# Weighing the values of two key blocks at a time in a fused attention stage, from six places for exponentials in place of four

## The reference

```python
x = x + 0.5 * moe(layernorm(x))          # top 2 of 8 experts, 256 -> 256 -> 256, silu gate
x = x + attention(layernorm(x))          # 16 heads of 16 features
x = x + 0.5 * moe(layernorm(x))

def attention(x):                        # 16 sequences of 1024 tokens
    latent = (x @ W_k + x @ W_v) @ W_down_kv
    q, k, v = x @ W_q, latent @ W_up_k, latent @ W_up_v
    scores = q @ k.T / sqrt(256) * exp(-0.01 * abs(tq - tk))
    return softmax(scores) @ v @ W_o
```

## Time and profile before

| what | value |
|---|---|
| median of 3 runs | 5893.35 us (5887.23 to 5893.88) |
| span of the profiled execution | 6207.9 us |
| the profiled execution's own time beside the span | not given by the page; the span is the whole of it |
| attention stage in it | from 1260 to 5157 us, 1024 W |
| TensorE busy, whole span | 5474.1 us (88%) |
| VectorE busy | 4582.3 us (74%) |
| ScalarE busy | 3294.6 us (53%) |
| GpSimd busy | 2823.2 us (45%) |

### The profile page before, as it was taken

How to read it: one execution, slowest core, us unless ns; L and a number is a source line. 1 busy time by engine, 2 the same in 40 slices (tenths; PEclk the granted TensorE clock), 3 DMA queues, 4 the chain that set the end, 5 groups by cost and what they waited for, 6 DMA issues and landing times.

```text
span 6207.9 us, 114160 instructions
## 1 busy us (share of the span) xinstructions
PE 5474.1 (88%) x35792; PEld 3260.2 (53%) x35792; DVE 4582.3 (74%) x14351; ACT 3294.6 (53%) x6557; POOL 2823.2 (45%) x2857
## 2 busy tenths in 40 slices
PE   4459999389999999999999999999999996988874
PEld 4448888134444444444444444444444444877763
DVE  6545555577888888888888888888888994545554
ACT  1124444156666666666666666666666664433321
POOL 5650000263656656647557566476574333012244
PEclk9999999689999999999999999999999997999987
DMA  4433333444545554545545555454454443335555
GB/s 152 147 109 105 105 105 102 130 100 89 122 104 113 127 102 117 117 101 121 117 106 123 110 114 123 100 122 113 104 122 96 97 75 121 105 112 160 157 180 171
DMA packets 535036, 728.64 MB, mean 117 GB/s; under 512 B 79892, under 2 KB 450740, under 8 KB 534452
## 3 DMA queue, kind: packets, MB, share of 16 engines
q1 hardware_dynamic: 485300, 587.06, 39.3%
q0 software_dynamic: 49152, 134.28, 7.3%
HBM read 425.64 MB, written 295.44 MB: 116 GB/s over the span
## 4 chain that ended last, share of the span: by engine, by line
PE 76%; DVE 10%; another core or an unknown queue 4%; issue 4%; POOL 3%; ACT 2%; DMA 1%; SPq 1%; DVEq 0%; ACTq 0%; POOLq 0%
PE psum L1312 15%; PE psum L1163 14%; PE psum L395 12%; PE psum L1172 11%; PE psum L412 6%; PE psum L1176 3%; PE psum L403 2%; DVE at_mx L1453 2%; PE psum L384 2%; PE psum L1288 2%; PE psum L1220 2%; ACT at_P L1376 1%; PE psum L1208 1%; PE psum L1230 1%
## 5 line engine op out<-in xcount | busy, mean ns | idle before, releaser
L1376 ACT ACTIVATE at_P<-psum 128x512 f32<-128x512 f32 x4096 | 2131.2, 602 | 1098.5 <-PE psum L1172 577.0
L1453 DVE TENSOR_REDUCE at_mx<-psum 128x4 f32<-128x512 f32 x3584 | 2220.2, 681 | 286.9 <-PE psum L1163 260.5
L1163 PE MATMUL psum<-at_kst,at_qst 96*128 96x128 bf16 (+3 forms) x7168 | 1599.1, 293 | 55.0 <-DVE at_mx L1453 28.8
L1172 PE MATMUL psum<-at_qst,at_kst 99*128 99x512 bf16 (+3 forms) x5120 | 1465.4, 319 | 100.8 <-ACT at_P L1376 96.1
L1163 PEld LDWEIGHTS psum<-at_kst,at_qst 96*128 96x128 bf16 x7168 | 616.3, 99 | 1326.5 <-DVE at_mx L1453 520.7
L1312 PE MATMUL psum<-at_P,at_V 128*17 128x512 f32 x8192 | 1095.2, 607 | 0.0
L1691 POOL TENSOR_TENSOR at_Sd<-at_Sd,at_m 128x1024 f32<-128x1024 f32 x256 | 484.4, 1898 | 886.8 <-DVE at_m L1462 885.9
L1172 PEld LDWEIGHTS psum<-at_qst,at_kst 99*128 99x128 bf16 x5120 | 490.5, 98 | 251.1 <-ACT at_P L1376 129.9
L1176 PE MATMUL psum<-at_ident,at_Sd 128*128 128x128 f32 x2048 | 565.1, 276 | 0.0
L696 POOL DMA_INDIRECT m2Y<-ys,m2yi x256 | 243.9, 953 | 692.2 <-DMA ys<-m2X 370.7
L1448 DVE CUSTOM_DVE_ANT_0 at_Sd<-psum,at_Dm 128x128 f32<-128x128 f32 x2048 | 444.9, 286 | 148.3 <-PE psum L1163 86.5
(11 more groups left out here) (267 smaller groups left out, 7893.0 us busy)
## 6 DMA issues: line engine op xcount, KB each, us to landing
parts<-at_pt SPq DMA_DIRECT2D x768, 128.0 KB
at_qst<-parts SPq DMA_DIRECT2D x768, 128.0 KB
at_kst<-parts SPq DMA_DIRECT2D x128, 384.0 KB
m2X<-xs SPq DMA_DIRECT2D x280, 128.0 KB
ys<-m2X SPq DMA_DIRECT2D x280, 128.0 KB
m1X<-xs SPq DMA_DIRECT2D x264, 128.0 KB
ys<-m1X SPq DMA_DIRECT2D x264, 128.0 KB
at_kst<-parts SPq DMA_DIRECT2D x128, 256.0 KB
```

Of the source, the lines that this page charges most:

```text
L1163: ins = e.matmul(bank[z % 4][:, col - 512 * u:col - 512 * u + ln], self.qst[0:96, s, side, 128 * t:128 * t + 128], self.kst[0:96, s, 1 - s ...
L1172: ins = e.matmul(turns[a % 3][:, q0 - 512 * qh:q0 - 512 * qh + ln], self.kst[0:99, s, side, 128 * kb:128 * kb + 128], self.qst[0:99, s, 1 ...
L1376: e.activation(self.P[:, i % NP, 512 * qh:512 * qh + 512], turns[a % 3], ACT.Exp).then_inc(self.taken.sem, 1)
L1453: e.tensor_reduce(self.mx[:, p % 2, hh, 8 * o + 4 * u:8 * o + 4 * u + 4], of, op=ALU.max, axis=AX.X).then_inc(self.s_read.sem, 1)
```

## The change

A W is done only behind every second step, and then for two blocks: `k = kb - 1` and `k = kb`, eight matmuls (16 records) in a row in place of four. In the numbers of the steps, a W stood behind every step `s` and now stands behind the even ones. `P` gets six places in place of four, so that three blocks of exponentials can be held. The count on the semaphore `weighed` is halved, and all waits on it are rewritten to it. Room for the two new places comes in part from `wk`, which no longer has memory of its own but lies in place 4 of `P` (it is used only while the stage is set up). No other work is moved in the list.

```diff
-    NS, NP, LEAD, DIAG = 3, 4, 4, 7
+    NS, NP, LEAD, DIAG = 3, 6, 4, 7
...
-        self.wq, self.wk, self.wo = sb("wq", [128, 2, D]), sb("wk", [128, 2, D]), sb("wo", [128, 2, D])
+        self.wq, self.wo = sb("wq", [128, 2, D]), sb("wo", [128, 2, D])
+        self.wk = self.P[:, 4, 0:512].rearrange("p (k d) -> p k d", k=2)
...
             if 0 < s <= 8 * NPAIR:
                 wp, wk = divmod(s - 1, 8)
-                yield ("W", wp, wk)
+                if wk % 2:
+                    yield ("W", wp, wk)
...
-                for hh in (1, 0):
-                    for qh in range(2):
-                        w.wait_ge(*self.result("T", p, kb, hh, qh))
-                        c = 32 * (2 * hh + qh)
-                        ins = e.matmul(V[c:c + 17, :], self.V[:, b % 2, kb, 2 * (p % 8) + hh, :],
-                                       self.P[:, self.p_slot(p, kb, hh) % NP, 512 * qh:512 * qh + 512], start=(kb == 0), stop=(kb == 7))
+                for k in (kb - 1, kb):
+                    for hh in (1, 0):
+                        for qh in range(2):
+                            w.wait_ge(*self.result("T", p, k, hh, qh))
+                            c = 32 * (2 * hh + qh)
+                            ins = e.matmul(V[c:c + 17, :], self.V[:, b % 2, k, 2 * (p % 8) + hh, :],
+                                           self.P[:, self.p_slot(p, k, hh) % NP, 512 * qh:512 * qh + 512], start=(k == 0), stop=(k == 7))
                 ins.then_inc(self.weighed.sem, 1)
...
                     i = self.p_slot(p, kb, hh)
-                    w.wait_ge(*self.weighed.at(i // 2 - 1))
+                    w.wait_ge(*self.weighed.at((i // 2 - NP // 2) // 2 + 1))
...
             if kind == "W" and at[1] == 7:
                 p = at[0]
-                w.wait_ge(*self.weighed.at(8 * p + 8))
+                w.wait_ge(*self.weighed.at(4 * p + 4))
```

More of the change, by code:

```diff
@@ L771, in __init__ @@
         self.m_max = sig.new("a_m_max", NPAIR)
-        self.weighed, self.ou_copied = sig.new("a_weighed", 8 * NPAIR), sig.new("a_ou_copied", NPAIR)
+        self.weighed, self.ou_copied = sig.new("a_weighed", 4 * NPAIR), sig.new("a_ou_copied", NPAIR)
         self.spread = sig.new("a_spread", B)
@@ L1067, in sync @@
         for dst, src in ((self.ident[:], cst["ident"]), (self.decay[:, 0], cst["decn"]), (self.decay[:, 1], cst["decp"]),
-                         (self.Dm[:], cst["dm"]), (self.wq[:], fold(wt["q"])), (self.wk[:], fold(wt["k"])),
+                         (self.Dm[:], cst["dm"]), (self.wq[:], fold(wt["q"])), (self.wk, fold(wt["k"])),
                          (self.wv, fold(wt["v"])), (self.wd[:], fold(wt["down"])), (self.wuk[:], wt["upk"]),
@@ L1121, in sync @@
             if kind == "next":
-                w.wait_ge(*self.weighed.at(8 * self.NPAIR))
+                w.wait_ge(*self.weighed.at(4 * self.NPAIR))
                 w.wait_ge(*self.x1_out.at(16 * B))
@@ L1352, in scalar @@
                 if b >= 2:
-                    w.wait_ge(*self.weighed.at(64 * (b - 1)))
+                    w.wait_ge(*self.weighed.at(32 * (b - 1)))
                 e.activation(self.V[:, b % 2, 2 * t2:2 * t2 + 2, :, 0:16], of[:, 0:512].rearrange("p (t h d) -> p t h d", t=2, h=H), ACT.Copy).then_inc(self.taken.sem, 1)
@@ L1396, in vector @@
         based = own.end(e.tensor_copy(base[:, 0, :], first[:, 0:E]))
-        e.tensor_tensor(self.wk[:], self.wk[:], self.wv, ALU.add).then_inc(self.w_ready.sem, 1)
+        e.tensor_tensor(self.wk, self.wk, self.wv, ALU.add).then_inc(self.w_ready.sem, 1)
         e.tensor_scalar_mul(self.wq[:], self.wq[:], 1.0 / 16.0).then_inc(self.w_ready.sem, 1)
```

## The result

The changed kernel takes 5960.48 us (median of 4 runs, 5951.15 to 5963.03) against 5892.54 for the kernel before on the same chip: a ratio of 1.0115, 95% interval 1.0103 to 1.0127. It is slower by 68 us; forecast were 5849, with a range of 5785 to 5900. A second set of runs, on another chip, gave 1.0124 (1.0107 to 1.0141).

A forecast was written before the change was run, and what follows sets the result against it. TensorE was taken to bound the attention stage. Drain saved -107, casts +84, late VectorE +25, shrinking stalls -26 and -20 sum to -44 us, so 5893 - 44 = 5849 us, range 5785 to 5900.

The forecast's parts named there:

- TensorE bounds the stage: Attention stage: TensorE busy 3735 of 3897 us, VectorE 12% behind it, so shortening TensorE's work shortens the stage.
- The drain: Entering and leaving the narrow strips around a W costs TensorE 0.21 us; 511 saved, 107 us less.
- Rival D: Double W: the second block's weight loads can't be hidden, so the drain stays between blocks; 6018 us, chance 0.04.
- Casts: 120 ScalarE casts behind odd steps lose the W's cover, making TensorE 0.70 us late each; 84 us more.
- VectorE behind at the start of even steps: Where statistics or maxima make VectorE late, some 65 pairs of steps lose their 0.21; 25 us more.
- Relief in odd steps: TensorE stalls behind odd steps shrink by up to 0.86 each, 26 us less; smaller ones give 20 less.
- the rank's longest wait: TensorE's wait for the routing's rank, once per sequence at an odd step's end, forecast down from 2.4 to 1.5.
- The clock stays: TensorE's granted clock in the attention stage remains 0.98, since work is as dense as before.
- Costed at nothing: Semaphore counts, the six places, wk in place 4, the copy after block 7 and mturn were priced at zero.
- plain steps can bear it: Steps without casts or late VectorE: VectorE needs 4.96 in 5.73 us per two steps; no stall.
- C, burst feeding stalls: VectorE's lateness isn't absorbed, 80 us in place of 25, no odd-step relief; 5950, chance 0.11 over the no-change band.
- the no-change band: Whole-kernel time within 0.2%, 12 us, about what a measurement can tell from no change; chance 0.10.

The follow-up runs named there:

- e13: Kernel before with maxima outside the diagonal block taken over only half the keys, so not the whole result; 5875.99 us.
- e14: Changed kernel with maxima outside the diagonal block taken over only half the keys, so not the whole result; 5873.52 us.
- e15: Kernel before with maxima over half the keys and only half of each cast done, so not the whole result; 5864.73 us.
- e16: Changed kernel with maxima over half the keys and only half of each cast done, so not the whole result; 5827.54 us.
- e2: Kernel before with six places in P and wk laid into P, but a W still behind each step; ratio 0.9998 to the kernel before.
- e7: Changed kernel with the first of each projection's two casts moved one step on, subtractions and sends left in their steps; 5921.23 us, ratio 1.0053 to the kernel before.
- e8: Control: kernel before with the first of each projection's two casts moved one step on; ratio 1.0008 to the kernel before.
- e9: Changed kernel with only mturn, the transpose of a pair's maxima, moved behind the double W; 5987.99 us, ratio 1.0165 to the kernel before.
- e10: Changed kernel with the double W straight behind the even step, ahead of all items due there; 6004.76 us, ratio 1.0184 to the kernel before.
- e11: Changed kernel with mturn behind the double W and the first cast moved one step on; 5949.47 us, ratio 1.0098 to the kernel before.
- e12: Changed kernel with the double W ahead of all items and the first cast moved one step on; 6019.56 us, ratio 1.0209 to the kernel before.
- e18: Changed kernel with 247 double W, single ones at maxima steps, before casts and at three more places per sequence; 5873.62 us, ratio 0.9976 to the kernel before.
- e1: Kernel before, unchanged, run for a second profile on a chip of the slower kind; 6205.87 us.
- e6: Kernel before, unchanged, traced on the same chip as the changed kernel's second trace; span 5891.7 us.

## Why the prediction was wrong

- *TensorE bounds the stage*: right for the kernel before, as the lightened kernels show (VectorE and ScalarE are busy for 86% and 67% of its stage, and cutting VectorE's busy time by a fifth wins 17 us).
- *The drain, 0.21 us a pair and 107 us in all*: right. 1.91 and 1.85 us came out as forecast, 107 us in the account. The rule of the Trainium skill that a change of tiling mode drains TensorE (TensorEngine Tiling (Array Packing), Key Properties) holds here, at 0.21 us. Rival D is refuted: had the second block's weight loads not been hidden, as the Trainium skill's rule on row groups has it (TensorE: Matmul & The Clock Gate, Part 3: Packing small matmuls — row/col tiling), the 16 records would last 2.1 us, D's own sign, and they last 1.91; the loads at 2932.41 and 2932.84 stand a whole pass ahead of their matmuls. The prediction read that section of the Trainium skill by one sentence alone: it also lets a load for the background weight buffer go ahead of running matmuls, and the trace agrees with that.
- *Casts, 84 us*: right in mechanism and size, 86.
- *VectorE behind at the start of even steps, 25 us*: 20. *Relief in odd steps, 46 us*: 54; the rank's longest wait fell from 2.4 to 1.8 and not to 1.5.
- *The clock stays*: 17 us went to the lower level.
- *The step that failed*: "Costed at nothing", with *plain steps can bear it*. It priced only the steps. mturn I looked at for the way of the maxima through memory, and not for the PSUM bank that it wants at once; `project`, `turn`, `out`, `oturn`, `norm` and `r_logits` behind even steps I did not price at all. These items stand where 1.07 us of cover had just been taken away, in front of the double W. By the account they cost 49 + 11 + 41 = 101 us where the sum had 0. Another 17 us went to the lower clock. The forecast terms themselves missed by a net 11 (+2 - 5 - 8). So -44 + 101 + 17 - 11 makes 63, and the stage grew by 62.
- *Range*: C, burst feeding stalls, was the right rival in kind, but that its 5950 lies near the measured 5960 is luck: it put its cost in VectorE's lateness at even steps (80 us, measured 20) and allowed no relief behind odd steps (measured 54). I gave it 0.21 with the no-change band, because the surplus in VectorE's work stands in front of the double W. That surplus helps in the odd step, as forecast, and hurts ahead of the W, which I missed.
- *Shown or argued*: that the length of VectorE's and ScalarE's work turns the gain into a loss is shown by e13 to e16; that memory and places cost nothing, by e2, on a chip of the other kind; that delays behind casts follow their place, by e7 with e8. That mturn, `project`, `norm` and part of `r_logits` wait for VectorE is shown by e14. How the 101 us divide over items is an account of one pair of traces, and e9 to e12 show that its parts can't be removed one by one. Three things stay open: what the 21 us of `turn`, `oturn` and `out` wait for one by one, why the clock was lower for longer, and why doubling at 17, 37 and 47 costs so much more than it had cost with all neighbours doubled.

## What to carry to other kernels

In this kernel work that keeps one engine busy without feeding the others was cover for them: putting two pieces of it together saved their fixed cost, but was paid by every consumer that needed the pause in between. Before grouping, list all that is queued between the pieces, items as well as loop steps, with the buffer each wants at once, and compare the pause with the depth of the rings: here 1.07 us of pause against three buffers that ScalarE takes in 0.5 us each and four that VectorE takes in 0.6 us each. And where a stall was the lateness of an engine that is 86% busy, moving the stalled item (e9, e10) made it worse; lightening that engine helped (e14), and so did grouping at fewer places (e18).

## What the runs showed of the hardware

- The same program takes some 5890 us on the chips of all other sets of runs and 6206 us in the set of e1, with the granted clock 0.969 and 0.952. A chip of that kind was met in this one set of runs and, it seems, in the first profile; that it is the chip and nothing else about that set is not shown. The windows view by stages, on that chip (e1) and on a faster one (e6):

```profile
0.00:1116.00 1116.00, 859.90 (x5250) 758.09 (x5250) 644.03 (x2396) 361.16 (x917) 274.41 (x298) 0.99 0.37 119
1116.00:5214.00 4098.00, 3834.04 (x26055) 1842.36 (x26055) 3401.76 (x10553) 2613.11 (x4796) 2265.57 (x2232) 0.96 0.50 110
5214.00:6204.00 990.00, 781.82 (x4487) 656.32 (x4487) 535.44 (x1403) 318.20 (x844) 278.16 (x328) 0.89 0.47 146
```

```profile
0.00:1059.00 1059.00, 857.78 (x5250) 757.80 (x5250) 647.44 (x2397) 363.80 (x917) 276.44 (x297) 0.99 0.39 126
1059.00:5065.00 4006.00, 3779.70 (x26055) 1821.42 (x26055) 3401.52 (x10552) 2605.26 (x4796) 2266.24 (x2232) 0.97 0.51 113
5065.00:5892.00 827.00, 733.02 (x4487) 632.51 (x4487) 532.09 (x1404) 327.06 (x844) 282.39 (x330) 0.94 0.56 175
```

  VectorE's and GpSimd's busy times agree within 2% in each stage; the last stage, which moves the most data per us, differs most (146 and 175 GB/s). In the attention stage the slower chip has 13 pauses of TensorE of 2.6 to 5 us, one in most sequences at the same step, that the faster one doesn't. A profile and the runs beside it need not be of one chip: stage times are to be compared only on one chip.
- Four matmuls of 17 columns in strips of 32 follow each other pass by pass at 0.43 us whether or not the accumulation moves on to the next weights, and entering and leaving the strips costs 0.09 and 0.12 us. In e6 a W starts 0.20 us (median of 248) after a diagonal transpose, and a score matmul 0.11 after one; behind the last pass the next matmul starts after 0.54 to 0.57 in 987 of 1023 cases, where pass follows pass after 0.43 to 0.44.
